# RWKV stage: the product exp(k)·v moved from GpSimd to VectorE, and the two carry scans swapped in order

## The chip, the cores and the metric

The kernel runs on all 8 cores of one Trainium2 chip, one batch element on each core, with no traffic between them. The metric is the device time of the slowest core in microseconds. In the profile the engines are called PE (TensorE matmul), PEld (TensorE weight load), DVE (VectorE), ACT (ScalarE), POOL (GpSimd) and SP (SyncE, which here only issues DMAs).

## The reference, cut to what matters

Two post-layernorm layers on x of shape (8, 2048, 1024): attention with ALiBi and a routed FFN, then RWKV time mixing and a second gated FFN. Only the RWKV part is touched.

```python
xx = jnp.pad(x, ((0, 0), (1, 0), (0, 0)))[:, :-1]
xk = x * time_mix_k + xx * (1.0 - time_mix_k)      # xv, xr alike
k = jnp.einsum('btc,dc->btd', xk, Wk)              # v from xv, Wv
sr = jax.nn.sigmoid(jnp.einsum('btc,dc->btd', xr, Wr))
w = -jnp.exp(time_decay)
# per step, up to a running rescale by exp(-p):
#   y = (a + e^(u+k) v) / (b + e^(u+k))
#   a = e^w a + e^k v ;  b = e^w b + e^k
rwkv = sr * _wkv(w, time_first, k, v)
return jnp.einsum('btd,cd->btc', rwkv, Wo)
```

The kernel works without the rescale: it computes e^k once, e^k·v once, and two linear recurrences over time.

## The kernel before

Channels lie on the 128 partitions (8 chunks `cc` of 128), time on the free axis. `l1_attn` walks the 2048 time steps in 4 blocks of 512. For each block:

- `emit_lerps(blk)` makes the mixed inputs of a block: for each chunk one difference (L952) and two fused multiply-adds (L973) on DVE, two operations (L997, L1002) on POOL.
- `emit_proj(blk, cc)` loads a slice of Wr (SP queue), runs 24 matmuls for K, V and R (L1027) into three PSUM banks of one parity, and evacuates them on ACT (L1034): `EKb` = exp(K), `VVb` = V, `SRBb` = sigmoid(R). Last it makes `EKVb` = `EKb`·`VVb` on POOL (L1038).
- `emit_scan(blk, cc)` does, all on DVE: copy of the carry (L1049), scan over `EKVb` into `Ab` (L1053), carry back (L1058); the same three for `Bb` over `EKb` (L1062, L1066, L1071); numerator `NUMb` (L1075, called n1 below) and denominator, written over `EKVb` (L1080, n2). Then ACT takes log and exp(-x) of the denominator into `EKb` (L1085, L1088), and POOL multiplies (L1091 into `NUMb`, called y1; L1095 into `RWK`, y2).
- `emit_outproj(blk)` multiplies by Wo: two halves, each with one load of `OTB` on the SP queue, 32 matmuls (L1115) into the two PSUM banks 6 and 7 in turn, and four additions to the residual `XR` on DVE (L1123).

`EKb`, `VVb`, `EKVb`, `Ab`, `Bb`, `NUMb` and `SRBb` have two buffers each, taken by the parity of `cc`; so the exp(K) of chunk cc+1 must wait until y1 of chunk cc-1 has read the `EKb` it writes.

Each engine executes its instructions in the order in which the Python emits them, and waits on semaphores at the head of its queue. The order of emission sets the queues around the change:

```python
emit_proj(blk, 0)
for cc in range(1, NC):
    emit_proj(blk, cc)
    if cc == 4 and blk > 0:
        emit_outproj(blk - 1)
    emit_scan(blk, cc - 1)
emit_scan(blk, NC - 1)
```

So the projection of chunk cc, with its product `EKVb`, stands ahead of the scans of chunk cc-1, and the eight residual additions of an output projection stand between the projection of chunk 4 and the scans of chunk 3. The lerps of block blk+1 are emitted ahead of all of block blk.

Of the kernel before, what the change touches and what calls it, by code (L numbers as in the profile page):

```python
# [12 lines left out]
ALU = mybir.AluOpType  # L13
# [126 lines left out]
class Build:  # L140
# [726 lines left out]
    def l1_attn(self, debug=False):  # L867
        em, nc = self.em, self.nc
# [10 lines left out]
        DCOL = self.sb("DCOL", [128, NC], F32, esL)  # L879
        EUCOL = self.sb("EUCOL", [128, NC], F32, esL)  # L880
        CAB = self.sb("CAB", [128, NC], F32, esL)
        CBB = self.sb("CBB", [128, NC], F32, esL)
# [5 lines left out]
        for cc in range(NC):  # L888
            a1 = em.op("scalar", lambda e, c=cc: e.activation(
                TCOL.ap[:], self.CP.ap[:, 56 + c:57 + c], AF.Exp),  # L890
                after=self.CP.rdeps() + TCOL.wdeps())
# [6 lines left out]
                after=[a2] + DCOL.wdeps())  # L898
# [3 lines left out]
                after=self.CP.rdeps() + EUCOL.wdeps())  # L902
# [107 lines left out]
        def emit_proj(blk, cc):  # L1010
            pp = blk % 2
            sp = cc % 2
            ekb, vv, ekv_b, srb = EKb[sp], VV[sp], EKV[sp], SRB[sp]
            rta = RTA[(blk * NC + cc) % 2]
            tr = em.dma("sync", lambda e, b=rta, c=cc: e.dma_start(
                out=b.ap[:], in_=rt_bf[:, c * 1024:(c + 1) * 1024]),
                after=rta.wdeps() + RTC.rdeps())
            RTC.read(tr)
            rta.wrote(tr)
            for pi, (wb, xin, outbuf, actf) in enumerate((  # L1020
                    (KTA, XK[pp], ekb, AF.Exp), (VTA, XV[pp], vv, AF.Identity),
                    (rta, XRr[pp], srb, AF.Sigmoid))):
                Pp = self.P[pi + 3 * sp]
                mm = None
                for kc in range(NC):
                    off = (cc * 1024 if wb in (KTA, VTA) else 0)
                    mm = em.op("tensor", lambda e, k=kc, w=wb, P=Pp, xi=xin, o=off: e.matmul(  # L1027
                        P.ap[:], w.ap[:, o + k * 128: o + k * 128 + 128],
                        xi[k].ap[:], start=(k == 0), stop=(k == NC - 1)),
                        after=(wb.rdeps() + xin[kc].rdeps() +  # L1030
                               (Pp.wdeps() if kc == 0 else [])))
                    wb.read(mm); xin[kc].read(mm)
                Pp.wrote(mm)
                ev = em.op("scalar", lambda e, P=Pp, o=outbuf, f=actf: e.activation(  # L1034
                    o.ap[:], P.ap[:], f),
                    after=Pp.rdeps() + outbuf.wdeps())
                Pp.read(ev); outbuf.wrote(ev)
            ekv = em.op("gpsimd", lambda e, a=ekv_b, x_=ekb, y_=vv: e.tensor_tensor(  # L1038
                a.ap[:], x_.ap[:], y_.ap[:], ALU.mult),
                after=ekb.rdeps() + vv.rdeps() + ekv_b.wdeps())  # L1040
            ekb.read(ekv); vv.read(ekv); ekv_b.wrote(ekv)

        def emit_scan(blk, cc):
            pp = blk % 2
            sp = cc % 2
            ekb, vv, ekv_b = EKb[sp], VV[sp], EKV[sp]
            ab, bb, num, srb = Ab[sp], Bb[sp], NUM[sp], SRB[sp]
            rwk = RWK[blk % 2]
            ca = em.op("vector", lambda e, c=cc, a=ab: e.tensor_copy(  # L1049
                a.ap[:, 0:1], CAB.ap[:, c:c + 1]),  # L1050
                after=CAB.rdeps() + ab.wdeps())
            CAB.read(ca); ab.wrote(ca)
            sa = em.op("vector", lambda e, c=cc, a=ab, x_=ekv_b: e.tensor_tensor_scan(  # L1053
                a.ap[:, 1:513], DCOL.ap[:, c:c + 1].to_broadcast([128, 512]),
                x_.ap[:], CAB.ap[:, c:c + 1], ALU.mult, ALU.add),
                after=[ca] + ekv_b.rdeps() + DCOL.rdeps() + CAB.rdeps() + ab.wdeps())
            DCOL.read(sa); CAB.read(sa); ekv_b.read(sa); ab.wrote(sa)
            ua = em.op("vector", lambda e, c=cc, a=ab: e.tensor_copy(  # L1058
                CAB.ap[:, c:c + 1], a.ap[:, 512:513]),
                after=[sa] + CAB.wdeps())  # L1060
            ab.read(ua); CAB.wrote(ua)
            cb = em.op("vector", lambda e, c=cc, a=bb: e.tensor_copy(  # L1062
                a.ap[:, 0:1], CBB.ap[:, c:c + 1]),
                after=CBB.rdeps() + bb.wdeps())
            CBB.read(cb); bb.wrote(cb)
            sb_ = em.op("vector", lambda e, c=cc, a=bb, x_=ekb: e.tensor_tensor_scan(  # L1066
                a.ap[:, 1:513], DCOL.ap[:, c:c + 1].to_broadcast([128, 512]),
                x_.ap[:], CBB.ap[:, c:c + 1], ALU.mult, ALU.add),
                after=[cb] + ekb.rdeps() + DCOL.rdeps() + CBB.rdeps() + bb.wdeps())
            DCOL.read(sb_); CBB.read(sb_); ekb.read(sb_); bb.wrote(sb_)  # L1070
            ub = em.op("vector", lambda e, c=cc, a=bb: e.tensor_copy(  # L1071
                CBB.ap[:, c:c + 1], a.ap[:, 512:513]),
                after=[sb_] + CBB.wdeps())
            bb.read(ub); CBB.wrote(ub)
            n1 = em.op("vector", lambda e, c=cc, a=ab, x_=ekv_b, n=num: e.scalar_tensor_tensor(  # L1075
                n.ap[:], x_.ap[:], EUCOL.ap[:, c:c + 1], a.ap[:, 0:512],
                ALU.mult, ALU.add),
                after=ekv_b.rdeps() + [sa] + EUCOL.rdeps() + num.wdeps())
            ekv_b.read(n1); ab.read(n1); EUCOL.read(n1); num.wrote(n1)
            n2 = em.op("vector", lambda e, c=cc, a=bb, x_=ekb, o=ekv_b: e.scalar_tensor_tensor(  # L1080
                o.ap[:], x_.ap[:], EUCOL.ap[:, c:c + 1], a.ap[:, 0:512],
                ALU.mult, ALU.add),
                after=[sb_, n1] + ekb.rdeps() + EUCOL.rdeps() + ekv_b.wdeps())
            ekb.read(n2); bb.read(n2); EUCOL.read(n2); ekv_b.wrote(n2)
            r1 = em.op("scalar", lambda e, x_=ekv_b, o=ekb: e.activation(  # L1085
                o.ap[:], x_.ap[:], AF.Ln), after=[n2] + ekb.wdeps())
            ekv_b.read(r1); ekb.wrote(r1)
            r2 = em.op("scalar", lambda e, o=ekb: e.activation(  # L1088
                o.ap[:], o.ap[:], AF.Exp, scale=-1.0), after=ekb.wdeps())
            ekb.wrote(r2)  # L1090
            y1 = em.op("gpsimd", lambda e, n=num, o=ekb: e.tensor_tensor(  # L1091
                n.ap[:], n.ap[:], o.ap[:], ALU.mult),
                after=[r2] + num.wdeps())
            ekb.read(y1); num.wrote(y1)
            y2 = em.op("gpsimd", lambda e, c=cc, n=num, s=srb, r=rwk: e.tensor_tensor(  # L1095
                r.ap[:, c * 512:(c + 1) * 512], n.ap[:], s.ap[:], ALU.mult),
                after=[y1] + srb.rdeps() + rwk.wdeps())
            num.read(y2); srb.read(y2); rwk.wrote(y2)
# [31 lines left out]
        for blk in range(NB_):  # L1130
            if blk + 1 < NB_:
                emit_lerps(blk + 1)
# [7 lines that stand above are left out]
# [239 lines left out]
```

How the kernel before makes its waits and increments, by code:

```python
            def body(e, _eng=eng_name):  # L103
                for (eng, waits, fn, inc) in self.q:
                    if eng != _eng:
                        continue
                    for (sem, v) in waits:
                        e.wait_ge(sem, v)
                    if fn is None:
                        continue
                    instr = fn(e)
                    if inc is not None:
                        instr.then_inc(*inc)
```

## Time and profile before

| | us |
|---|---|
| the two runs shown | 3562.12 and 3644.55, median 3603.33 |
| profiled execution, device time | 3559.92 |
| its span on the slowest core (core 3) | 3558.3 |
| spans of the eight cores | 3520.5 to 3558.3 |
| layer 0 (0 to about 1990) | attention, layernorm, FFN |
| layernorm, then RWKV lerps of blocks 0 and 1 | 1990 to 2199 |
| RWKV scans of blocks 0 to 3 | 2199 to 2565 |
| last output projection | 2565 to 2595 |
| layernorm and second FFN | 2595 to 3558 |

An engine's queue is read from the timeline view: start and duration of each instruction (or of a run of alike ones), the line, the tile written and the tiles read, and in square brackets the idle time ahead of it with what ended it. Durations marked as one number for "x8" or "x32" are for the run of instructions together.

### The profile page before, as it was taken

The page shows a single profiled execution, that of the slowest core. Times are in us where ns is not written, and L with a number is a line of the kernel's source. Part 1 is how long each engine was busy: PE and PEld are TensorE (multiplying, and loading weights), DVE is VectorE, ACT ScalarE, POOL GpSimd, SP SyncE. Part 2 cuts the span into 40 slices and gives each one's busy share as a digit, 9 for nine tenths or more (in the row PEclk, how much of TensorE's full clock was granted, in tenths as well). Part 3 has the DMA queues.
Part 4 walks back from the last instruction along what each step waited for, and adds up shares of the span by engine and source line. Part 5 has one row for each costly group of instructions (what it writes and reads, how often), then busy time and mean ns, then how long its engine had stood idle before and what let it go on. Part 6 is the DMA issues. An engine that isn't in the chain of part 4 may idle for free.

```text
span 3558.3 us, 28694 instructions; the slowest of 8 cores (3520.5 to 3558.3 us)
## 1 busy us (share of the span) xinstructions
PE 2241.3 (63%) x7902; PEld 827.2 (23%) x7902; DVE 1246.2 (35%) x1905; ACT 945.6 (27%) x1370; POOL 598.4 (17%) x592
## 2 busy tenths in 40 slices
PE   2677667776766437786968424566534869687842
PEld 1222222222222112232423101222201323232310
DVE  0233333333332643001010378876564310110155
ACT  0064446444642211020201122444421102010111
POOL 0000000000000330000000156654333000000024
PEclk9867876677677668897989656788856889898965
DMA  6100000000001026798989305111103689999822
GB/s 162 24 1 7 7 7 1 7 7 4 4 1 24 1 48 107 132 170 139 164 150 162 66 9 106 30 48 33 48 12 58 109 141 166 151 159 155 152 46 94
DMA packets 48179, 258.71 MB, mean 73 GB/s; under 512 B 4647, under 2 KB 13160, under 8 KB 20510
## 3 DMA queue, kind: packets, MB, share of 16 engines
q0 software_dynamic: 32256, 222.35, 36.6%
q1 hardware_dynamic: 15726, 34.44, 2.9%
q8 instruction: 74, 1.21, 0.1%
q14 instruction: 75, 0.61, 0.1%
q10 hardware_dynamic: 48, 0.10, 0.0%
HBM read 470.76 MB, written 12.60 MB: 136 GB/s over the span
## 4 chain that ended last, share of the span: by engine, by line
PE 41%; DMA 18%; DVE 16%; issue 8%; ACT 7%; POOL 6%; another core or an unknown queue 2%; DVEq 0%; ACTq 0%; POOLq 0%; SPq 0%
PE P L797 9%; PE P L820 6%; DMA W2B<-W2g 5%; PE P L469 5%; PE P L497 5%; DMA X1B<-W1g 4%; PE P L437 4%; DMA W1B<-W1g 4%; PE P L838 4%; ACT PBt L478 4%; DMA X2B<-W2g 4%; PE P L1115 2%; PE P L371 2%; PE P L573 2%
## 5 line engine op out<-in xcount | busy, mean ns | idle before, releaser
L478 ACT ACTIVATE PBt<-P,BSP 128x512 bf16<-128x512 f32 x640 | 408.0, 692 | 412.1 <-PE P L469 407.9
L805 ACT ACTIVATE HB<-P,CP 128x512 bf16<-128x512 f32 x256 | 175.9, 687 | 1001.3 <-PE P L797 991.8
L497 PE MATMUL P<-PBt,VT 128*65 128x512 bf16 x640 | 320.8, 505 | 92.4 <-DVE PBt L486 77.4
L469 PE MATMUL P<-QA,KA 67*128 67x512 bf16 x640 | 308.3, 517 | 8.1 <-DVE KA L446 8.0
L797 PE MATMUL P<-XB,X1B 128*128 128x512 bf16 x1024 | 254.2, 395 | 41.1 <-DMA X1B<-W1g 40.6
L797 PE MATMUL P<-XB,W1B 128*128 128x512 bf16 x1024 | 254.1, 394 | 39.9 <-DMA W1B<-W1g 39.8
L486 DVE TENSOR_TENSOR PBt<-PBt,M 128x512 bf16<-128x512 bf16 x256 | 109.0, 426 | 337.0 <-ACT PBt L478 336.6
L761 DVE SCALAR_TENSOR_TENSOR F0T<-P,CP,GBF 128x512 f32<-128x512 f32 x32 | 23.9, 747 | 537.0 <-PE P L820 325.1
L1205 DVE SCALAR_TENSOR_TENSOR F1T<-P,CP,XR 128x512 f32<-128x512 f32 x32 | 23.9, 747 | 511.8 <-PE P L820 319.7
L838 PE MATMUL P<-HB,W2B 128*128 128x512 bf16 x384 | 131.3, 512 | 109.8 <-DMA W2B<-W2g 101.6
L838 PE MATMUL P<-HB,X2B 128*128 128x512 bf16 x384 | 131.7, 512 | 104.3 <-DMA X2B<-W2g 93.2
L1027 PE MATMUL P<-XB,KTA 128*128 128x512 bf16 x256 | 76.0, 446 | 161.0 <-ACT EKb L1034 106.7
L245 PE MATMUL P<-XB,OC 128*1 128x512 bf16 x128 | 71.6, 560 | 164.5 <-DVE XB L321 97.3
L820 PE MATMUL P<-HB,W2B 128*128 128x512 bf16 x640 | 161.1, 385 | 5.8 <-DMA W2B<-W2g 5.7
L820 PE MATMUL P<-HB,X2B 128*128 128x512 bf16 x640 | 161.6, 386 | 3.2 <-DMA X2B<-W2g 3.0
L497 PEld LDWEIGHTS P<-PBt,VT 128*65 128x65 bf16 x640 | 84.4, 132 | 326.5 <-issue 326.1
L797 PEld LDWEIGHTS P<-XB,X1B 128*128 128x128 bf16 x1024 | 102.3, 101 | 177.5 <-issue 69.9
L797 PEld LDWEIGHTS P<-XB,W1B 128*128 128x128 bf16 x1024 | 102.0, 101 | 176.3 <-issue 68.2
L405 POOL DMA_DIRECT2D WQB<-Wqh x8 | 4.2, 527 | 689.1 <-PE P L437 646.9
L437 PE MATMUL P<-XB,WQB 128*128 128x512 bf16 x256 | 86.8, 500 | 48.6 <-DVE QA L451 41.5
L371 PE MATMUL P<-WVbf,XB 128*128 128x512 bf16 x256 | 60.5, 402 | 74.9 <-DMA WVbf<-Wvh 74.9
L1115 PE MATMUL P<-RWK,OTB 128*128 128x512 bf16 x256 | 66.3, 424 | 52.5 <-DMA OTB<-ot_bf 28.0
(259 smaller groups left out, 3033.4 us busy)
## 6 DMA issues: line engine op xcount, KB each, us to landing
W2B<-W2g POOLq DMA_DIRECT2D x64, 1024.0 KB, 10.3
X2B<-W2g POOLq DMA_DIRECT2D x64, 1024.0 KB, 10.2
W1B<-W1g POOLq DMA_DIRECT2D x32, 1024.0 KB, 13.7
X1B<-W1g POOLq DMA_DIRECT2D x32, 1024.0 KB, 13.7
XR<-xT SPq DMA_DIRECT2D x8, 1024.0 KB
RTA<-rt_bf SPq DMA_DIRECT2D x32, 256.0 KB
OTB<-ot_bf SPq DMA_DIRECT2D x8, 1024.0 KB
yT<-XR SPq DMA_DIRECT2D x8, 1024.0 KB
```

Source lines behind the costliest of these rows:

```text
L371: mt = em.op("tensor", lambda e, k=kc, ti=tile, P=Pv: e.matmul(P.ap[:], self.XB[k].ap[:, ti * 128:(ti + 1) * 128], WV.ap[:, k * 512:(k + 1 ...
L437: mm = em.op("tensor", lambda e, k=kc, w=wbuf, P=Ps, c=col: e.matmul(P.ap[:], w.ap[:, k * 128:(k + 1) * 128], self.XB[k].ap[:, c:c + 512], ...
L469: kb=ka, qb=qa: e.matmul(P.ap[:], kb.ap[0:67, k * 128:(k + 1) * 128], qb.ap[0:67, q:q + 512], start=True, stop=True),
L478: tex = em.op("scalar", lambda e, P=psc, b=pb, bc=bcol: e.activation(b.ap[:], P.ap[:], AF.Exp, scale=0.125, bias=BSP.ap[:, bc:bc + 1]), af ...
L486: tmk = em.op("vector", lambda e, b=pb, jj=j: e.tensor_tensor(b.ap[:], b.ap[:], M01.ap[:, jj * 512:(jj + 1) * 512], ALU.mult), after=pb.wd ...
L497: f=first, l=last: e.matmul(P.ap[0:65, :], VT.ap[:, (k * H + hh) * 65:(k * H + hh) * 65 + 65], b.ap[:], start=f, stop=l),
L797: mm = em.op("tensor", lambda e, k=kc, q=hq, P=Ph, b=w1b, c=col: e.matmul(P.ap[:], b.ap[:, q * 1024 + k * 128: q * 1024 + k * 128 + 128], ...
L805: ev = em.op("scalar", lambda e, P=Ph, h=hc: e.activation(HBc[h].ap, P.ap[:], act, bias=self.CP.ap[:, b1_off + h:b1_off + h + 1], scale=1. ...
L820: mm = em.op("tensor", lambda e, q=hq, o=oc, b=w2b, h=hc, Pp=P: e.matmul(Pp.ap[:], b.ap[:, q * 1024 + o * 128: q * 1024 + o * 128 + 128], ...
L838: mm = em.op("tensor", lambda e, q=hq, o=oc, b=w2b, h=hc, Pp=P: e.matmul(Pp.ap[:], b.ap[:, q * 1024 + o * 128: q * 1024 + o * 128 + 128], ...
L1027: mm = em.op("tensor", lambda e, k=kc, w=wb, P=Pp, xi=xin, o=off: e.matmul(P.ap[:], w.ap[:, o + k * 128: o + k * 128 + 128], xi[k].ap[:], ...
L1115: mm = em.op("tensor", lambda e, c=cc, o=oi, Pp=Po, r=rwk: e.matmul(Pp.ap[:], OTB.ap[:, c * 512 + o * 128: c * 512 + o * 128 + 128], r.ap[ ...
```

## The change

Two edits, both in `l1_attn`. In `emit_proj` the product `EKVb` = `EKb`·`VVb` is issued on VectorE and no longer on GpSimd. In `emit_scan` the three instructions of the `Bb` recurrence stand ahead of the three of the `Ab` recurrence. Their text is otherwise the same, and nothing else moves.

```diff
-            ekv = em.op("gpsimd", lambda e, a=ekv_b, x_=ekb, y_=vv: e.tensor_tensor(
+            ekv = em.op("vector", lambda e, a=ekv_b, x_=ekb, y_=vv: e.tensor_tensor(
                 a.ap[:], x_.ap[:], y_.ap[:], ALU.mult),
                 after=ekb.rdeps() + vv.rdeps() + ekv_b.wdeps())
@@ emit_scan
             rwk = RWK[blk % 2]
+            cb = em.op("vector", lambda e, c=cc, a=bb: e.tensor_copy(
+                a.ap[:, 0:1], CBB.ap[:, c:c + 1]),
+                after=CBB.rdeps() + bb.wdeps())
+            CBB.read(cb); bb.wrote(cb)
+            sb_ = em.op("vector", lambda e, c=cc, a=bb, x_=ekb: e.tensor_tensor_scan(
+                a.ap[:, 1:513], DCOL.ap[:, c:c + 1].to_broadcast([128, 512]),
+                x_.ap[:], CBB.ap[:, c:c + 1], ALU.mult, ALU.add),
+                after=[cb] + ekb.rdeps() + DCOL.rdeps() + CBB.rdeps() + bb.wdeps())
+            DCOL.read(sb_); CBB.read(sb_); ekb.read(sb_); bb.wrote(sb_)
+            ub = em.op("vector", lambda e, c=cc, a=bb: e.tensor_copy(
+                CBB.ap[:, c:c + 1], a.ap[:, 512:513]),
+                after=[sb_] + CBB.wdeps())
+            bb.read(ub); CBB.wrote(ub)
             ca = em.op("vector", lambda e, c=cc, a=ab: e.tensor_copy(
...
             ab.read(ua); CAB.wrote(ua)
-            (the same ten lines of cb, sb_ and ub, which stood here)
             n1 = em.op("vector", lambda e, c=cc, a=ab, x_=ekv_b, n=num: e.scalar_tensor_tensor(
```

## Rows read from the trace of the kernel before

**Rows 1.** Windows view: us, busy by engine, granted PE clock, DMA share, GB/s.
```profile
2199.00:2565.00 366.00, 216.86 (x884) 90.01 (x882) 259.04 (x329) 168.07 (x214) 180.50 (x127) 0.81 0.14 41
```

**Rows 2.** Waits, 2199 to 2595: engine, line, waited for: us in total, times, longest.
```profile
ACT L1085 <- DVE Ab L1049: 134.1, 7, 32.1
...
PE P L1027 <- ACT EKb L1034: 106.7, 19, 30.7
```

**Rows 3.** Timeline, ACT, one step of block 0: start, us, instruction.
```profile
2219.34 0.60 ACT L1034 ACTIVATE EKb<-P 128x512 f32<-128x512 f32 x1 [1.57 <-PE P L1027]
2219.84 0.59 ACT L1034 ACTIVATE VVb<-P 128x512 f32<-128x512 f32 x1
2220.89 1.28 ACT L1034 ACT_TABLE_LOAD   x1 [0.46 <-POOL RWK L1095]
2222.18 0.60 ACT L1034 ACTIVATE SRBb<-P 128x512 bf16<-128x512 f32 x1
2222.80 1.28 ACT L1085 ACT_TABLE_LOAD   x1
2224.09 0.63 ACT L1085 ACTIVATE EKb<-EKVb 128x512 f32<-128x512 f32 x1
2224.81 0.63 ACT L1088 ACTIVATE EKb<-EKb 128x512 f32<-128x512 f32 x1
2227.00 0.60 ACT L1034 ACTIVATE EKb<-P 128x512 f32<-128x512 f32 x1 [1.56 <-POOL NUMb L1091]
```

**Rows 4.** Timeline, POOL, the same step.
```profile
2219.39 1.42 POOL L1095 TENSOR_TENSOR RWK<-NUMb,SRBb 128x512 bf16<-128x512 f32 x1
2220.77 1.71 POOL L1038 TENSOR_TENSOR EKVb<-EKb,VVb 128x512 f32<-128x512 f32 x1
2225.64 1.26 POOL L1091 TENSOR_TENSOR NUMb<-NUMb,EKb 128x512 f32<-128x512 f32 x1 [3.16 <-DVE Bb L1066]
```

**Rows 5.** Timeline, DVE, the same step: denominator beside y2, scan behind the product.
```profile
2219.90 1.46 DVE L1080 SCALAR_TENSOR_TENSOR EKVb<-EKb,EUCOL,Bb 128x512 f32<-128x512 f32 x1
...
2222.58 1.28 DVE L1053 TENSOR_TENSOR_SCAN Ab<-DCOL,CAB,EKVb 128x512 f32<-128x512 f32 x1 [1.16 <-POOL EKVb L1038]
```

**Rows 6.** Timeline, DVE, block 1: first and last residual addition, scans of chunk 3.
```profile
2315.82 0.69 DVE L1123 TENSOR_TENSOR XR<-XR,P 128x512 f32<-128x512 f32 x1 [1.11 <-PE P L1115]
...
2336.88 0.69 DVE L1123 TENSOR_TENSOR XR<-XR,P 128x512 f32<-128x512 f32 x1 [1.04 <-PE P L1115]
2337.48 0.15 DVE L1049 COPY Ab<-CAB 128x1 f32<-128x1 f32 x1
...
2341.89 0.75 DVE L1080 SCALAR_TENSOR_TENSOR EKVb<-EKb,EUCOL,Bb 128x512 f32<-128x512 f32 x1
```

**Rows 7.** Timeline, ACT, block 1: exp(K) of chunk 2; the log that waits; chunk 5.
```profile
2305.03 0.60 ACT L1034 ACTIVATE EKb<-P 128x512 f32<-128x512 f32 x1 [1.84 <-POOL NUMb L1091]
...
2342.71 1.28 ACT L1085 ACT_TABLE_LOAD   x1 [19.18 <-DVE Ab L1049]
2344.01 0.63 ACT L1085 ACTIVATE EKb<-EKVb 128x512 f32<-128x512 f32 x1
...
2347.36 0.60 ACT L1034 ACTIVATE EKb<-P 128x512 f32<-128x512 f32 x1 [2.00 <-PE P L1027]
```

**Rows 8.** Timeline, DVE, two differences of the lerps: POOL idle, POOL busy.
```profile
2259.73 0.68 DVE L952 TENSOR_TENSOR DDl<-XR 128x512 f32<-128x512 f32 x1
...
2261.91 1.76 DVE L952 TENSOR_TENSOR DDl<-XR 128x512 f32<-128x512 f32 x1
```

**Rows 9.** Timeline, PE, block 1: projections of chunk 4, then the output projection.
```profile
2305.77 3.57 PE L1027 MATMUL P<-XB,KTA 128*128 128x512 bf16 x8 [30.70 <-ACT EKb L1034]
2309.14 3.13 PE L1027 MATMUL P<-XB,VTA 128*128 128x512 bf16 x8
2312.10 1.89 PE L1027 MATMUL P<-XRr,RTA 128*128 128x512 bf16 x8
2313.82 7.07 PE L1115 MATMUL P<-RWK,OTB 128*128 128x512 bf16 x32
2327.39 9.38 PE L1115 MATMUL P<-RWK,OTB 128*128 128x512 bf16 x32 [6.49 <-DMA OTB<-ot_bf]
```

**Rows 10.** Timeline, DVE, start of block 1 behind the lerps.
```profile
2292.09 0.14 DVE L1049 COPY Ab<-CAB 128x1 f32<-128x1 f32 x1
2294.61 2.20 DVE L1053 TENSOR_TENSOR_SCAN Ab<-DCOL,CAB,EKVb 128x512 f32<-128x512 f32 x1 [2.38 <-POOL EKVb L1038]
...
2299.60 0.75 DVE L1080 SCALAR_TENSOR_TENSOR EKVb<-EKb,EUCOL,Bb 128x512 f32<-128x512 f32 x1
```

**Rows 11.** Timeline, ACT (chunks 2 and 7 of block 0), DVE (last denominators of blocks 0, 1).
```profile
2211.67 0.60 ACT L1034 ACTIVATE EKb<-P 128x512 f32<-128x512 f32 x1 [1.61 <-POOL NUMb L1091]
...
2250.13 0.60 ACT L1034 ACTIVATE EKb<-P 128x512 f32<-128x512 f32 x1 [1.56 <-POOL NUMb L1091]
...
2258.34 1.46 DVE L1080 SCALAR_TENSOR_TENSOR EKVb<-EKb,EUCOL,Bb 128x512 f32<-128x512 f32 x1
...
2370.62 1.46 DVE L1080 SCALAR_TENSOR_TENSOR EKVb<-EKb,EUCOL,Bb 128x512 f32<-128x512 f32 x1
```

More of the change, by code:

```diff
@@ L1061, in emit_scan @@
             ab.read(ua); CAB.wrote(ua)
[L1062 to L1074, printed above, removed]
             n1 = em.op("vector", lambda e, c=cc, a=ab, x_=ekv_b, n=num: e.scalar_tensor_tensor(
```

## The prediction
> **What bounds the kernel now.** The windows view comes first, to find what share of the span the change can touch. The scan part of the RWKV stage is 366 of 3558.3 us, and in it DVE is busy 259, PE 217, POOL 181 and ACT 168 [rows 1]. No engine is full, so this part is bound by who waits for whom. The waits view says that ACT's log (L1085) stands 134 us, nearly all of it at seven places, and that PE stands 107 us for ACT to empty a PSUM bank [rows 2]: PE follows, it doesn't lead.
>
> Then the timeline, for the loop that repeats. Call E the start of exp(K) of chunk cc on ACT. After it ACT does V, a table load, sigmoid, a table load, log and exp(-x) of chunk cc-1, and then stands until y1 of chunk cc-1 has ended on POOL; the next exp(K) starts at E+7.66 (2227.00 - 2219.34) [rows 3]. The reader is to see two things. The second table load starts 0.02 us after the sigmoid with no wait: the denominator of chunk cc-1 was done at 2221.36 (2219.90 + 1.46), 1.4 us before ACT came to ask for it [rows 3, 5]. So DVE has slack here, and ACT with y1 behind it (1.26 us) is the loop [rows 4]. And DVE stands 1.16 us for POOL's product, then begins the scans of chunk cc while ACT and POOL are still busy with chunk cc-1 [rows 5]: the overlap of neighbouring chunks rests on the product being on another queue than the scans.
>
> **The change, part by part.** Removed: 32 products from POOL, 1.71 us each in the step read [rows 4]. Added: 32 on DVE. The nearest DVE instruction with two float32 inputs in SBUF and the same shape takes 0.68 us with POOL idle and 1.76 with POOL busy [rows 8]; y2 of the chunk before runs from E+0.05 to E+1.47 in the old step [rows 4], the product can start at about E+1.2, so I take 0.7 us (end at E+1.9) and keep 1.76 as the upper bound.
>
> What counts is where it stands in the queue. The product of chunk cc is emitted ahead of the scans of chunk cc-1. It needs V, which ends at E+1.09 (0.50 + 0.59) [rows 3]. Behind it on DVE stand both scans, n1 and n2 of chunk cc-1, for n2 the log waits on ACT, for the log y1, and for y1 exp(K) of chunk cc+1. So the loop becomes a single chain:
>
> - E to the end of the product: 1.9.
> - Six carry and scan instructions, n1 and n2 with POOL idle: from 2337.48 to 2342.64, 5.16 [rows 6]. The order of the two recurrences doesn't alter it, as all stand behind the product; swapping them is costed at nothing. With the first small copy issued 0.07 before the product's end, n2 ends at E+7.0.
> - Log: the table load starts only when the wait is over (19.18 idle, then the load, then 1.30 later the log) [rows 7]. It was behind the sigmoid before. Here the wait ends at E+7.0, long after the sigmoid (about E+3.2). Take 0.2 to the load, 1.30 to the log, 0.72 to exp, 0.63 for it, 0.2 to y1 (2225.64 against 2225.44), 1.26 for it, 0.1 to the next exp(K): 4.4 [rows 3, 4, 7].
>
> The step is then 1.9 + 5.1 + 4.4 = 11.35 instead of 7.66, 3.7 more. At a block's end, n2 of chunk 7 now follows n2 of chunk 6 rather than its own product: 7.0 + 5.1 + 1.3 for n1 and n2 standing behind y1 and y2 (1.46 beside y2 against 0.75 alone, twice [rows 5, 6]) = E+13.35; before it was E+9.67 (2259.80 - 2250.13) [rows 11].
>
> On DVE beside POOL the rows show 1.46 for n2 beside y2 and 0.75 for it alone [rows 5, 6]. The Trainium skill, SBUF — State Buffer, "SBUF: two separate sides", has it that a two-input DVE instruction and a POOL instruction hold a shared port pair exclusively, the later one waiting. By that rule the product starts behind y2 and ends at about E+2.0, 0.1 us later per step, which would put 2 us on the total; it excludes a full 1.76 unless POOL is at work all along, and this trace agrees with it (n2 ends 0.55 behind y2).
>
> Block 0. The start gains: DVE was free at the first copy and stood 2.38 us for POOL, which had the lerps and two products to do [rows 10] (these are of block 1; block 0 reads alike). Now two products behind the lerps (POOL's last lerp operation covers about 1.1 of it) end about 2.5 after the first copy, then 5.1: n2 at +7.55 against 8.26 (2300.35 - 2292.09), a gain of 0.7. From E of chunk 2 to n2 of chunk 7 it was 48.13 (2259.80 - 2211.67) [rows 11]; it becomes 5 x 11.35 + 13.35 = 70.1, 22.0 more. Net +21.3.
>
> Blocks 1 to 3 have the output projection. The eight residual additions stand behind the product of chunk 4. E of chunk 4 comes 2 x 11.35 = 22.7 after E of chunk 2 (2305.03 in block 1 [rows 7]), the product ends at 24.6, against a first addition at 10.8 before [rows 6]. PE computes two output chunks early, fills banks 6 and 7, and stands for about 13 us. It restarts at 25.4; after a long idle, eight matmuls took 3.57 us and the next eight 3.13, against 1.72 a group in the flow [rows 9], so the first half ends at about 31.7 (28.9 if the clock stays up). `OTB` can only be reloaded then: 6.5 to the next matmul, and 10.1 from there to the first copy of chunk 3's scans (2337.48 - 2327.39) [rows 6, 9]. That is 48.3 after E of chunk 2, against 32.45 before: +15.85. The projection of chunk 5 is behind it on PE but ready in time, 5.2 us of matmuls against 9.9 to E of chunk 5. That stretch loses contention, -0.3. From E of chunk 5 to n2 of chunk 7: 24.72 before (2372.08 - 2347.36 [rows 7, 11]), now 2 x 11.35 + 13.35 = 36.05: +11.3. With the start's -0.7 a block gives +26.15. Block 3 has no lerps ahead of it and gains nothing at its start: +26.85.
>
> Nothing behind hides it: the last output projection waits for the last y2, and a barrier follows. Sum: 21.3 + 2 x 26.15 + 26.85 = 100.4. Against this execution's own 3559.92 that is **3660 us, +2.8%**. That execution is close to the lower run shown (3562.12) and 1.2% under the median of 3603.33; the upper run (3644.55) is 2.3% above the lower, and with it as base the same sum gives 3745.
>
> **The rivals.**
>
> *Contention stays.* If the product takes 1.76 and not 0.7, that is 1.06 x 24 (six of the eight products in each block lie on the chain) = 25: 3686. For it: each DVE row beside POOL is long. Against: POOL is idle from E+1.5 on.
>
> *The table load costs more when exposed.* The Trainium skill, ScalarE: Activation LUTs, "What ACT_TABLE_LOAD costs", adds about 1.38 us of drain to a load of 1.28. Here the rows show the load 0.02 behind the sigmoid and the log 0.01 behind the load [rows 3]. As a mechanism of this kernel: each of the 17 newly exposed loads (5 in block 0, 4 in each other block) costs one table load more, 17 x 1.28 = 22: 3682.
>
> *The load is not exposed.* If the load ran while ACT waits, -22: 3638. Against: the load behind a 19.18 us wait [rows 7].
>
> *The other sign: hidden anyway.* DVE had idle time, and POOL lets go of it. It needs n2 of chunk cc-1 done by the time the sigmoid is, E+3.2. Then the loop stays at 7.66, the starts gain 0.7 x 3, and the time is 3558. For it: 1.4 us of slack, 1.16 of DVE standing for POOL [rows 5]. Against: it only holds if the scans of chunk cc-1 can run ahead of the product of chunk cc, and DVE's queue is in order; from V's end to E+3.2 there are 2.1 us for 5.8 us of work.
>
> **How the numbers follow.** Forecast 0.70, contention 0.09, dearer load 0.04, load not exposed 0.05, hidden 0.08, something else 0.04. Within the forecast the clock moves it: 3 x 2.8 = 8 us less if the first halves run at full clock, some 12 more if second halves run at the lower level. With the cheaper load and half of the clock's gain it starts at 3634, with the contention and the slower clock it ends at 3698; the distance of the two runs shown can carry it to 3745. The range is 3634 to 3745, leaving out the hidden case and little more. A measurement of this kernel tells about 2% from no change, 71 us. Slower by over 2%: 0.64 of the forecast, the two dearer cases 0.13, half of the cheaper one, most of the rest, 0.82. Within 2%: 0.06 + 0.02 + 0.06 + 0.02 = 0.16. Faster: 0.02, from the hidden case.
>
> **What would show it.** In the profile after: exp(K) to exp(K) 11.3 us in block 0; ACT idle some 4 us ahead of every log's table load, released by DVE; the product on DVE near 0.7; PE standing about 13 us inside the first half of each output projection, for a residual addition; POOL's products gone, its idle time up. The scan part should last about 466 us rather than 366, and the rest of the span be unchanged. It is wrong if the step stays near 7.7 (the chain isn't single), if it is near 12.4 (contention) or 10.1 (load ahead of the wait), or if the additions start as early as before.

## The result, and the profile after

The changed kernel takes 3655.18 us (median of 11 runs) against 3561.49 for the kernel before, run beside it: ratio 1.0275, 95% interval 1.0262 to 1.0288, slower by 98 us. Where a second, slower level of the chip shows in some runs of either kernel (up to 3778 us here), ratios compare only the undisturbed runs, which is why 98 us is more than the distance of the two medians, 94. The forecast was 3660 us, +2.8%.

The windows view of the changed kernel comes first, cut at the end of the lerps ahead of block 0, at the last scans, and at the last residual addition. The columns are as in [rows 1]: after the length of the stretch, the busy time of PE, PEld, DVE, ACT and POOL with the number of instructions, then the granted PE clock, the DMA share and GB/s.

```profile
2200.45:2667.00 466.55, 239.25 (x882) 95.03 (x879) 249.37 (x361) 167.65 (x214) 125.91 (x95) 0.74 0.10 32
2667.00:2697.00 30.00, 18.25 (x64) 7.12 (x64) 5.51 (x8) 1.02 (x2) 2.41 (x2) 0.77 0.11 35
2697.00:3657.60 960.60, 598.95 (x2255) 227.15 (x2255) 280.74 (x441) 145.56 (x223) 175.75 (x194) 0.78 0.63 114
```

The scan part went from 366.0 [rows 1] to 466.55 us: all of the loss is in it. The parts around it are nearly what they were (30.0 both times, and 960.6 against 963.3 us). Within it DVE is busy for less time than before, 249 against 259 us, although it has 32 more instructions: POOL works beside it less often (n2 takes 0.75 us in the step below and 1.46 in [rows 5]). So the engine that got the work has not become full. The waits view (2199 to 2697) says where the time is:

```profile
POOL NUMb L1091 <- ACT EKb L1088: 322.9, 30, 34.4
ACT L1085 <- DVE EKVb L1080: 227.4, 24, 31.1
...
DVE EKVb L1038 <- ACT VVb L1034: 140.0, 26, 5.9
```

ACT's log stood for 134 us at seven places before [rows 2]; now the line shown has 24 places and 227 us. The view splits such waits by name. With its other rows (4 and 4 places now, 3 and 1 before) all 32 logs stand for VectorE, against 11 before. The last line is new: VectorE stands 26 times, 140 us, at the head of its queue for the V of the next chunk. The timeline of one step of block 0 shows that the engines take turns (DVE first, then ACT, then POOL; small copies left out):

```profile
2224.48 0.69 DVE L1038 TENSOR_TENSOR EKVb<-EKb,VVb 128x512 f32<-128x512 f32 x1 [5.54 <-ACT VVb L1034]
...
2225.34 1.28 DVE L1053 TENSOR_TENSOR_SCAN Bb<-DCOL,CBB,EKb 128x512 f32<-128x512 f32 x1
...
2229.40 0.75 DVE L1080 SCALAR_TENSOR_TENSOR EKVb<-EKb,EUCOL,Bb 128x512 f32<-128x512 f32 x1
2235.68 0.69 DVE L1038 TENSOR_TENSOR EKVb<-EKb,VVb 128x512 f32<-128x512 f32 x1 [5.53 <-ACT VVb L1034]
```

```profile
2223.23 0.60 ACT L1034 ACTIVATE EKb<-P 128x512 f32<-128x512 f32 x1 [1.56 <-POOL NUMb L1091]
2223.72 0.59 ACT L1034 ACTIVATE VVb<-P 128x512 f32<-128x512 f32 x1
2224.51 1.28 ACT L1034 ACT_TABLE_LOAD   x1 [0.20 <-POOL RWK L1095]
2225.80 0.60 ACT L1034 ACTIVATE SRBb<-P 128x512 bf16<-128x512 f32 x1
2230.23 1.28 ACT L1085 ACT_TABLE_LOAD   x1 [3.83 <-DVE EKVb L1080]
2231.52 0.63 ACT L1085 ACTIVATE EKb<-EKVb 128x512 f32<-128x512 f32 x1
2232.24 0.63 ACT L1088 ACTIVATE EKb<-EKb 128x512 f32<-128x512 f32 x1
2234.43 0.60 ACT L1034 ACTIVATE EKb<-P 128x512 f32<-128x512 f32 x1 [1.56 <-POOL NUMb L1091]
```

```profile
2223.28 1.15 POOL L1095 TENSOR_TENSOR RWK<-NUMb,SRBb 128x512 bf16<-128x512 f32 x1
2233.07 1.26 POOL L1091 TENSOR_TENSOR NUMb<-NUMb,EKb 128x512 f32<-128x512 f32 x1 [8.64 <-ACT EKb L1088]
```

Exp(K) to exp(K) is 11.20 us (2234.43 - 2223.23), against 7.66 in [rows 3]. The load ahead of the log, which followed the sigmoid at once, now stands 3.83 us for DVE. The product takes 0.69 us and ends 1.94 us after exp(K) starts (2225.17 - 2223.23).

In block 1, at the output projection, the first addition (DVE) and the matmuls (PE) read:

```profile
2350.12 1.28 DVE L1123 TENSOR_TENSOR XR<-XR,P 128x512 f32<-128x512 f32 x2
...
2372.53 0.69 DVE L1123 TENSOR_TENSOR XR<-XR,P 128x512 f32<-128x512 f32 x1 [1.04 <-PE P L1115]
```

```profile
2333.00 3.62 PE L1115 MATMUL P<-RWK,OTB 128*128 128x512 bf16 x16
2350.95 6.46 PE L1115 MATMUL P<-RWK,OTB 128*128 128x512 bf16 x16 [14.33 <-DVE XR L1123]
2363.81 8.62 PE L1115 MATMUL P<-RWK,OTB 128*128 128x512 bf16 x32 [6.40 <-DMA OTB<-ot_bf]
```

The same windows view, with PE alone, gives the granted clock of the two groups of 16 matmuls (the number behind the busy time):

```profile
2333.00:2336.62 3.62, 3.62 (x17) 1.00 0.00 0
2350.95:2357.41 6.46, 6.45 (x16) 0.55 0.00 0
```

PE fills its two banks, stands 14.33 us for an addition that is queued behind the product of chunk 4, and restarts mostly at the lower of its two clock levels (granted 0.55 of the full clock, 6.46 us, against 1.00 and 3.62). Only then can the second half of `OTB` be loaded.

### The profile page after: what moved, and what is told of

It reads as the page before. It is cut to its first block, busy times and chain, and to the rows that moved or that the text cites. A ratio compares the mean times of both kernels' runs of the same rounds, so it can differ in the third digit from the quotient of the medians.

```text
span 3657.6 us, 28647 instructions; the slowest of 8 cores (3616.8 to 3657.6 us)
## 1 busy us (share of the span) xinstructions
PE 2267.9 (62%) x7902; PEld 833.7 (23%) x7902; DVE 1235.4 (34%) x1937; ACT 947.5 (26%) x1370; POOL 543.8 (15%) x560
## 4 chain that ended last, share of the span: by engine, by line
PE 41%; DVE 18%; DMA 17%; ACT 8%; issue 8%; POOL 4%; another core or an unknown queue 2%; DVEq 1%; ACTq 0%; POOLq 0%; SPq 0%
PE P L797 10%; PE P L820 6%; PE P L469 5%; PE P L497 5%; DMA X1B<-W1g 4%; DMA W1B<-W1g 4%; PE P L437 4%; DMA X2B<-W2g 4%; DMA W2B<-W2g 4%; ACT PBt L478 3%; PE P L838 3%; PE P L1115 2%; PE P L371 2%; PE P L573 2%
## 5 line engine op out<-in xcount | busy, mean ns | idle before, releaser
L1027 PE MATMUL P<-XB,KTA 128*128 128x512 bf16 x256 | 88.7, 504 | 187.0 <-ACT EKb L1034 132.7
L1115 PE MATMUL P<-RWK,OTB 128*128 128x512 bf16 x256 | 73.9, 458 | 105.0 <-DVE XR L1123 42.5
L437 PE MATMUL P<-XB,WQB 128*128 128x512 bf16 x256 | 86.9, 501 | 48.3 <-DVE QA L451 41.5
## 6 DMA issues: line engine op xcount, KB each, us to landing
X1B<-W1g POOLq DMA_DIRECT2D x32, 1024.0 KB, 12.6
```

The costliest lines, as they stand in the source:

```text
L437: mm = em.op("tensor", lambda e, k=kc, w=wbuf, P=Ps, c=col: e.matmul(P.ap[:], w.ap[:, k * 128:(k + 1) * 128], self.XB[k].ap[:, c:c + 512], ...
L1115: mm = em.op("tensor", lambda e, c=cc, o=oi, Pp=Po, r=rwk: e.matmul(Pp.ap[:], OTB.ap[:, c * 512 + o * 128: c * 512 + o * 128 + 128], r.ap[ ...
```

## The experiments

The theory: the loss comes from the product's place in VectorE's in-order queue, ahead of the scans of the chunk before. The rivals: the order of the two recurrences; the work added to VectorE; the helper lost on GpSimd and the contention between the two; and, for the size, the activation tables.

**The swap alone.** The changed kernel with the product back on GpSimd.

```diff
-            ekv = em.op("vector", lambda e, a=ekv_b, x_=ekb, y_=vv: e.tensor_tensor(
+            ekv = em.op("gpsimd", lambda e, a=ekv_b, x_=ekb, y_=vv: e.tensor_tensor(
```

> Only the swap of the two recurrences; the product stays on GpSimd. Queue theory (the cost is the product's place in VectorE's queue): the step from exp(K) to exp(K) stays at 7.66 us, since VectorE has slack there; at the start of blocks 0 to 2 the Bb scan (1.8 us) now runs while VectorE stands 2.4 us for the product, so 1.7 us less each, about -5 us, ratio 0.9985. Rival (the order of the recurrences carries part of the cost): slower by 10 us or more.

Measured: ratio 0.999, interval 0.9945 to 1.0036. The swap costs nothing that can be measured. The interval holds the expected -5 us (0.9985), so the gain is not shown, and also the rival's +10 us (1.0028), so the time alone does not exclude it; the profile speaks against it. The steps of block 0 were 8.1, 8.0, 7.4, 8.0 and 7.7 us rather than a steady 7.7: the first scan no longer waits for the product, and now runs beside it.

```profile
2212.58 1.71 POOL L1038 TENSOR_TENSOR EKVb<-EKb,VVb 128x512 f32<-128x512 f32 x1
2213.41 1.97 DVE L1053 TENSOR_TENSOR_SCAN Bb<-DCOL,CBB,EKb 128x512 f32<-128x512 f32 x1 [0.17 <-DVE Bb L1049]
```

The scan takes 1.97 us where 1.28 is the duration alone. The expectation had the gain at the wrong place. In the profiled execution the start of block 0 gains 0.9 us rather than 1.7 (7.42 from the first copy to the first denominator, against 8.29). The end of each block gains about 3 (exp(K) of chunk 7 to its denominator 6.5 to 6.8 us, against 9.6 to 9.7 [rows 11]), since the last scans start earlier. The scan part is 7.4 us shorter than in the kernel before (357.8 against 365.2, from the first copy to the last denominator). That is one execution of each kernel, and the device time doesn't resolve it.

**The product alone.** The kernel before with only that line's engine changed. It was run a second time for an interval.

```diff
-            ekv = em.op("gpsimd", lambda e, a=ekv_b, x_=ekb, y_=vv: e.tensor_tensor(
+            ekv = em.op("vector", lambda e, a=ekv_b, x_=ekb, y_=vv: e.tensor_tensor(
```

> Only the product on VectorE, Ab recurrence first as before. Queue theory: the whole loss, step about 11.2 us, +95 to +100 us over the kernel before, ratio 1.027 to 1.028. Rival (the order matters once the product is on VectorE): clearly different from the changed kernel, by 10 us or more (32 scans that could trade places for about 0.3 us each).

> The product on VectorE without the swap once more, for an interval: ratio 1.026 to 1.029, the same as the changed kernel's 1.0275, so the swap carries nothing.

Measured: 3656 us for the fastest of the first runs, and ratio 1.0278 (1.0228 to 1.0329) in the second set; the step is 11.2 us. The product carries the whole loss, and beside it the order of the recurrences changes nothing that can be measured: 1.0275 with the swap, and the same steps of 11.2 us with it and without.

**The same work at another place in the queue.** The changed kernel, with the product emitted as the first instruction of its own `emit_scan`.

```diff
@@ emit_proj, at its end
-            ekv = em.op("vector", ...)
-            ekb.read(ekv); vv.read(ekv); ekv_b.wrote(ekv)
@@ emit_scan
             rwk = RWK[blk % 2]
+            ekv = em.op("vector", ...)
+            ekb.read(ekv); vv.read(ekv); ekv_b.wrote(ekv)
             cb = em.op("vector", lambda e, c=cc, a=bb: e.tensor_copy(
```

> The changed kernel with one difference: the product of chunk cc, still on VectorE, is emitted at the head of the scans of chunk cc instead of at the end of its projection. Same instructions on the same engines. Queue theory: the scans of chunk cc-1 run ahead of it again, the step falls back to between 7.4 and 7.7 us, ratio 0.994 to 1.001 against the kernel before (3540 to 3565 us). Rival (work added to VectorE): 32 x 0.69 = 22 us stay, ratio 1.006. Rival (losing GpSimd as a helper, port contention): 1.01 to 1.03.

Measured: ratio 0.9985 (0.9954 to 1.0016). Same instructions on the same engines, and the 98 us are gone; 1.006 for the added work and 1.01 for the lost helper both lie outside the interval. ACT's steps in block 0:

```profile
2213.89 0.60 ACT L1034 ACTIVATE EKb<-P 128x512 f32<-128x512 f32 x1 [1.85 <-PE P L1027]
...
2217.35 1.28 ACT L1085 ACT_TABLE_LOAD   x1
...
2222.10 0.60 ACT L1034 ACTIVATE EKb<-P 128x512 f32<-128x512 f32 x1 [2.10 <-POOL NUMb L1091]
...
2229.63 0.60 ACT L1034 ACTIVATE EKb<-P 128x512 f32<-128x512 f32 x1 [1.70 <-POOL NUMb L1091]
```

The load ahead of the log has no wait again. The denominator of the chunk before ends ahead of the next product now:

```profile
2220.13 0.75 DVE L1080 SCALAR_TENSOR_TENSOR EKVb<-EKb,EUCOL,Bb 128x512 f32<-128x512 f32 x1
2220.20 1.81 POOL L1091 TENSOR_TENSOR NUMb<-NUMb,EKb 128x512 f32<-128x512 f32 x1 [4.83 <-DVE NUMb L1075]
2223.28 0.69 DVE L1045 TENSOR_TENSOR EKVb<-EKb,VVb 128x512 f32<-128x512 f32 x1 [2.40 <-ACT VVb L1034]
```

The step is 8.2 and 7.5 us in the two shown, 7.4 to 8.2 in block 0, not the 7.4 to 7.7 expected: y1 takes 1.81 us beside the denominator, where it takes 1.26 alone. VectorE's 22 us of new work and the lost helper cost nothing that can be measured.

**The wait without the work.** The kernel before, product on GpSimd, with a copy of one column of V on VectorE where the change put the product.

```diff
             ekb.read(ekv); vv.read(ekv); ekv_b.wrote(ekv)
+            dv = em.op("vector", lambda e, y_=vv: e.tensor_copy(
+                TCOL.ap[:], y_.ap[:, 0:1]), after=vv.rdeps() + TCOL.wdeps())
+            vv.read(dv); TCOL.wrote(dv)
```

> The kernel before, product on GpSimd, with a copy of one column of V (128x1) on VectorE in the place in the queue where the change put the product; its result is not used. Queue theory: the wait alone is enough; the scans of chunk cc-1 start behind V of chunk cc and now also beside GpSimd's product; step 11.2 to 11.7 us, +90 to +115 us, ratio 1.025 to 1.032. Rival (the added work): 32 x 0.15 = 5 us, ratio 1.001.

Measured: ratio 1.0286 (1.0201 to 1.0371). The DVE timeline of one step:

```profile
2227.24 0.15 DVE L1042 COPY TCOL<-VVb 128x1 f32<-128x1 f32 x1 [5.47 <-ACT VVb L1034]
2227.31 0.14 DVE L1052 COPY Ab<-CAB 128x1 f32<-128x1 f32 x1
2227.63 2.06 DVE L1056 TENSOR_TENSOR_SCAN Ab<-DCOL,CAB,EKVb 128x512 f32<-128x512 f32 x1 [0.17 <-DVE Ab L1052]
...
2238.63 0.15 DVE L1042 COPY TCOL<-VVb 128x1 f32<-128x1 f32 x1 [5.47 <-ACT VVb L1034]
```

A copy of 0.15 us makes the step 11.39 us (2238.63 - 2227.24) and costs as much as the whole change. This shows the mechanism: it is the wait, not the work. The step is 0.2 longer than in the changed kernel: the first scan runs beside GpSimd's product and takes 0.78 more (2.06 against 1.28), and the copy ends 0.54 earlier than a product would (0.15 against 0.69).

**One activation table, changed kernel.** The sigmoid of R is replaced by exp; the gate is then not the reference's.

```diff
-                    (rta, XRr[pp], srb, AF.Sigmoid))):
+                    (rta, XRr[pp], srb, AF.Exp))):
```

> The changed kernel with the sigmoid of R replaced by exp, so that the RWKV loop needs one activation table only and no table load stands in it (the gate is computed wrongly). Queue theory with the load exposed: the step loses exactly the one load on the chain, 11.2 - 1.28 = 9.9 us, though two loads a step vanish; about 24 exposed loads, -31 us, 3621 us, ratio to the kernel before 1.016 to 1.020. Rival (the loads are hidden, or the switch costs a drain of 1.4 us beside the load): step 11.2, or 8.5 and -65 us.

Measured: 3625.34 us, ratio 1.0208 (1.0158 to 1.0258), a little above the ratio expected and 4 us from the expected time. The step:

```profile
2228.59 0.60 ACT L1034 ACTIVATE EKb<-P 128x512 f32<-128x512 f32 x1 [1.56 <-POOL NUMb L1091]
...
2235.61 0.63 ACT L1085 ACTIVATE EKb<-EKVb 128x512 f32<-128x512 f32 x1 [5.12 <-DVE EKVb L1080]
...
2238.52 0.60 ACT L1034 ACTIVATE EKb<-P 128x512 f32<-128x512 f32 x1 [1.56 <-POOL NUMb L1091]
```

9.93 us, so 1.27 less: the one load on the chain. Two loads a step vanished, and the one behind V was covered. An exposed switch costs the load of 1.28 us and no more. The scan part bears out the expected count of 24 loads, six in a block (7.7 us): from last denominator to last denominator, blocks 0 and 1 are 7.65 and 7.55 us shorter than in the changed kernel. Blocks 2 and 3 are 8.65 and 13.26 shorter; there the output projections ran faster too.

**One activation table, kernel before.** The same edit to the kernel before.

> The kernel before with the same replacement of sigmoid by exp. The step of 7.66 us holds two loads on ACT (2.56 us); without them VectorE becomes the loop: its 5.2 us of work a chunk, 6.5 with contention, or the way from the denominator of chunk cc-2 to the product of chunk cc, 6.0. Step 6.0 to 6.6 us, -20 to -30 us, ratio 0.992 to 0.995. The distance from the changed kernel with the same replacement should then be about the same as with sigmoid, 85 to 105 us: the added step length (3.7) does not come from the tables alone. Rival (the loss comes from the tables): the distance shrinks to half.

Measured: ratio 0.9987 (0.9955 to 1.002), a miss: -20 to -30 us was expected. The step fell only to 7.16 us (2255.53 - 2248.37 on ACT), not to 6.0 to 6.6. VectorE is now the loop: it has hardly any idle time left and works beside POOL most of the time, so that its instructions are long:

```profile
2247.38 1.98 DVE L1066 TENSOR_TENSOR_SCAN Bb<-DCOL,CBB,EKb 128x512 f32<-128x512 f32 x1 [0.17 <-DVE Bb L1062]
...
2249.53 1.33 DVE L1075 SCALAR_TENSOR_TENSOR NUMb<-EKVb,EUCOL,Ab 128x512 f32<-128x512 f32 x1
2250.96 1.57 DVE L1080 SCALAR_TENSOR_TENSOR EKVb<-EKb,EUCOL,Bb 128x512 f32<-128x512 f32 x1
...
2252.77 1.29 DVE L1053 TENSOR_TENSOR_SCAN Ab<-DCOL,CAB,EKVb 128x512 f32<-128x512 f32 x1 [0.17 <-DVE Ab L1049]
```

That is where the expected gain went. There are 17 plain steps (5 in block 0, 4 in each of the others): 17 x 1.1 to 1.7 us would have been 19 to 28, and 17 x 0.5 is 8.5. The scan part of the profiled execution is 6.2 us shorter (359.0 against 365.2); the ends of the blocks gave some back (10.5 us from exp(K) of chunk 7 to its denominator in block 0, against 9.67).

The distance between this and its counterpart is 71 us by the medians (3625.3 - 3554.0) and 79 by the ratios (0.0221 of 3558, give or take 21), against 98 with sigmoid. So the distance lies above half of 98, which was the rival, but the device times alone can't tell it from the 85 to 105 expected. In the profiles the scan parts are 70 us apart (429.1 - 359.0), against 101 with sigmoid (466.2 - 365.2). In the plain steps the change adds 2.77 us (9.93 - 7.16) and not 3.54, 13 us less in 17 steps. The rest lies mostly in the output projections and was not taken apart; there the granted clock counts, and it was lower in this run (0.758 over the span of the profiled core, 0.777 in the kernel before). So the tables account for roughly a fifth to a third of the loss, as part of the length of the single chain, and not for its being single: some 70 us stay without them.

**The product of chunk 4 back on GpSimd**, in the changed kernel, for the output projection's share.

```diff
-            ekv = em.op("vector", lambda e, a=ekv_b, x_=ekb, y_=vv: e.tensor_tensor(
+            ekv = em.op("gpsimd" if cc == 4 else "vector", lambda e, a=ekv_b, x_=ekb, y_=vv: e.tensor_tensor(
```

> The changed kernel with the product of chunk 4 alone back on GpSimd. Queue theory: the residual additions of the output projection no longer stand behind the product of chunk 4 but behind the scans of chunk 2, which end at E(chunk 3)+7.0; the first addition comes 18 us after exp(K) of chunk 2 instead of 24.6, -6 us in each of blocks 1 to 3, and one step of block 0 is 7.7 instead of 11.2. Together -21.5 us against the changed kernel: 3634 us, ratio to the kernel before 1.019 to 1.023. Rival (the output projection's part is the matmul clock or the weight load, not the place of the additions): -4 us at most, ratio 1.026.

Measured: 3634.2 us, ratio 1.0219 (1.0195 to 1.0243), which lies below the changed kernel's interval. In block 1 the exp(K) of chunk 2 and the first additions:

```profile
2317.33 0.60 ACT L1034 ACTIVATE EKb<-P 128x512 f32<-128x512 f32 x1 [1.56 <-POOL NUMb L1091]
...
2335.34 1.28 DVE L1123 TENSOR_TENSOR XR<-XR,P 128x512 f32<-128x512 f32 x2
```

18.0 us between them instead of 24.6, as expected: the output projection is late by what is queued ahead of its additions. The rival (the clock or the weight load, -4 us at most) had ratio 1.026, outside the interval.

**A version that beats both.** The order of the third experiment, and the weights of the output projection in four quarters and two buffers; and, to part the two, the quarters alone in the kernel before. The diff shows the loops only; the tile and the column numbers change to match.

```diff
-            for oh in range(2):
+            for oh in range(4):
+                OTB = OTQ[oh % 2]
                 tw = em.dma("sync", ...)      # a quarter: all chunks, 256 columns
...
-                for oi in range(4):
+                for oi in range(2):
```

> A candidate: the product at the head of its own scans, and the weights of the output projection loaded in four quarters into two buffers of half the size instead of two halves into one buffer, so that a quarter lands while the one before is used. The kernel before stands 6.5, 7.0, 8.2 and 6.4 us on PE for the second half. Each should shrink to 0 to 3 us: -18 to -26 us, ratio 0.993 to 0.995 against the kernel before. Rival (the loads are issued late or the quarters are too small to hide): ratio 0.998 to 1.000.

> The candidate once more for an interval: product on VectorE at the head of its own scans, quarters. 3520 to 3535 us, ratio 0.991 to 0.994. If the product's engine matters beside the quarters, this and the kernel before with quarters differ by more than 5 us; expected is no difference that can be measured.

> The kernel before with the four quarter loads of the output projection's weights and nothing else. The profile of the version with the product at its scans and the quarters shows the gap around each output projection down by about 8 us (18.2 to 18.9 against 26 to 27 us from exp(K) of chunk 4 to exp(K) of chunk 5). Expected here: the same, 3 x 8 + 6 at the end = -30 us, ratio 0.991 to 0.993; and the step stays at 7.66 us against 7.9 there.

Measured: the first set gave no interval (median 3538, lowest 3519); the second 3530 us, ratio 0.990 (0.985 to 0.995). The quarters alone: 3540 us, ratio 0.9937 (0.9905 to 0.9969), a little short of the 0.991 to 0.993 expected, which the interval holds. Both beat the kernel before, by 0.6 to 1%. Their medians are 10 us apart, but their intervals overlap, so the time can't tell them from each other, and their scan parts last the same within 1 us (332.7 and 333.6 from the first denominator to the last, 356.9 in the kernel before). Nothing shows that the new place of the product adds to the quarters. On PE of block 1, quarters alone:

```profile
2315.28 7.07 PE L1116 MATMUL P<-RWK,OTB 128*128 128x512 bf16 x32
2323.51 7.10 PE L1116 MATMUL P<-RWK,OTB 128*128 128x512 bf16 x31 [1.16 <-DMA OTB<-ot_bf]
```

The 6.49 us in the middle [rows 9] are 1.16, and the second half runs in 7.1 us rather than 9.38: its granted clock is 1.00 where it was 0.75, and PE stood for 1.16 us ahead of it and not for 6.49.

## Why the prediction was right, point by point

- **The step.** Forecast 11.35 (its terms, 1.9 + 5.1 + 4.4, add to 11.4), measured 11.16 to 11.21, with 11.5 three times. The product ends at E+1.94 (1.9 forecast), the 5.16 of scans and n1, n2 measured 5.06 (2225.09 to 2230.15), and from there to the next exp(K) it is 4.28 (4.4 forecast). Whether the product waits for y2, as one reading in the prediction has it, this step can't tell: y2 had become shorter and ended at 2224.43, 0.12 behind V, and the product started at 2224.48. The wait-only run shows that the position is the cause.
- **End of a block.** From E of chunk 2 to n2 of chunk 7 in block 0: 70.1 forecast, 69.6 measured (2281.63 - 2212.07).
- **Starts.** n2 of chunk 0 ends 7.3 us behind the lerps in blocks 0 to 2, forecast 7.55: a gain of 1.0, not 0.7. Block 3 has no lerps, and its start was put at nothing. It lost 1.5: n2 of chunk 0 came 12.6 us behind the last n2 of block 2, against 11.1 before, since the product of chunk 1 now stands ahead of the scans of chunk 0 as well.
- **Output projection.** First addition at 24.6 after E of chunk 2 in block 1, forecast and measured (2350.12 - 2325.55). The start of chunk 3's scans came at 47.6 against 48.3. The clock fell as supposed: the 16 matmuls took 6.46 us in block 1 against 6.3 in the sum (4.96 and 6.42 in blocks 2 and 3). No row gives that 6.3; the two groups of eight that the prediction names add to 6.7. The step with the output projection grew by 7.2, 9.6 and 11.0 us in blocks 1 to 3 (34.22, 34.46 and 36.92 against 27.01, 24.85 and 25.88), where the sum has about 8.2 each time.
- **Block 1's tail**, E of chunk 5 to n2 of chunk 7: 36.05 forecast, 35.65 measured (2418.13 - 2382.48).
- **The swap at nothing.** Beside the product on VectorE it holds: 1.0275 with the swap, 1.0278 without. Alone it is 0.999, and its small gain in the profile is not resolved by the time.
- **The rivals.** Contention fell (0.69 for the product). The dearer load fell (1.27 less when it is gone). The load ran behind its wait in all 28 places where the log has one (24 and 4 rows of the waits view), so the cheaper load fell. Nothing was hidden.

The mechanism was right. That the total came within 1 us is in part luck. From the last denominator of a block to that of the next (in block 0 from the end of the lerps) the four blocks grew by 20.3, 24.2, 26.5 and 30.0 us, against 21.3, 26.15, 26.15 and 26.85 in the sum: 3 us too much in the first two blocks cancel 3.5 too little in the last two. The sum is 101.0 against 100.4 forecast, and the scan part was forecast at 466 us and measured 466.55. The profiled execution took 3659.18, 99.3 more than the 3559.92 from which the forecast started; 4 of the 5 us between 3660 and the median of 3655 are only the distance of that execution from the median.

## What to carry to other kernels

Before an instruction is moved to another engine, ask what it waits for and what stands behind it in the new queue. Here the engine had slack and the operation became faster (0.69 us against 1.26 to 1.71), and it still cost 98 us, because it made the engine wait for chunk cc before it would finish chunk cc-1. The cure was the place of emission, not the engine: an operation that is moved to the consumer's engine belongs with the consumer.

## What the runs showed of the hardware that was not expected

A scan over 128x512 float32 takes 1.28 us alone. When it started while a GpSimd instruction was running, it always ended 1.07 to 1.09 us behind the end of that instruction, whatever was left of it: 94 scans in all the traces kept here, 1.42 to 2.38 us long. In the rows shown for the swap alone the product ends at 2214.29 and the scan at 2215.38. Of the 738 other scans all but one took 1.28 or 1.29 us; the exception (2.37 us) started 0.03 ahead of a y1 and ended 1.08 behind it. So on these rows such a scan does its work only when GpSimd has finished, and the cost depends on how much of the GpSimd instruction was left.

It goes the other way too. y1 on GpSimd takes 1.26 us alone, and when it started while n1 or n2 was running, it ended 1.11 to 1.14 us behind that instruction, 58 times in these traces: n2 ends at 2220.88 in the rows of the third experiment, y1 at 2222.01. Moving the same instructions by a microsecond made single steps 7.4 to 8.2 us long where they had been 7.7. Over block 0 these differences nearly cancel for the swap alone: its five steps add to 39.2 us, against 38.5.
